# Routed experts in pairs of slots: full 128-row chunks, two 64-row remainders in two row tiles, and eight result buffers

## What is computed

```
x = x + cross_attention(layernorm(x), ctx)          # 16 heads of 16, q, k and the output normalised
h = layernorm(x)
scores = sigmoid(h @ W_gate_router)                 # 8 experts
sel = top_2(scores + expert_bias)
w = scores[sel] / sum(scores[sel])
shared = silu(h @ Wg_s) * (h @ Wu_s) @ Wd_s         # inner width 192
routed = sum over the 2 chosen e: w_e * (silu(h @ Wg[e]) * (h @ Wu[e]) @ Wd[e])   # inner width 192
x = x + shared + routed
```

## Time and profile before

| what | value |
|---|---|
| median of 3 runs | 596.49 us |
| the profiled execution | 595.83 us |
| its span, first to last instruction | 594.0 us |
| TensorE matmul busy (PE) | 502.4 us, 85% |
| VectorE busy (DVE) | 344.9 us, 58% |
| ScalarE busy (ACT) | 238.7 us, 40% |
| GpSimd busy (POOL) | 244.4 us, 41% |
| mean granted TensorE clock | 0.942 |
| L975, the `up` matmuls | 288 records, 106.1 us |
| L991, the `down` matmuls | 288 records, 74.4 us |
| L531, the scatters | 72, 111.1 us |

### The profile page before, as it was taken

One profiled execution on the slowest core, in us unless ns is written; L12 is line 12 of the kernel. 1 busy time (PEld: TensorE's weight loads), 2 busy tenths in 40 slices (PEclk: granted clock), 3 DMA queues, 4 the chain that ended last, 5 costly groups with the idle time before them and its releaser, 6 DMA issues.

```text
span 594.0 us, 10983 instructions
## 1 busy us (share of the span) xinstructions
PE 502.4 (85%) x2876; PEld 288.6 (49%) x2877; DVE 344.9 (58%) x1032; ACT 238.7 (40%) x468; POOL 244.4 (41%) x218
## 2 busy tenths in 40 slices
PE   4836989999888888856798998399999999999990
PEld 3724334444444443312454454166667666667660
DVE  5775547767888687415657933045555555555550
ACT  0255778888777777524222101022222222222210
POOL 5353411112111832361026657235565636655644
PEclk9956999999999999988799999699999999999996
DMA  8911901111111310121534652436575656664733
GB/s 284 357 44 63 290 20 37 36 38 52 37 37 36 116 66 37 55 81 46 176 100 159 216 202 77 132 49 110 75 118 93 91 99 95 98 116 75 113 52 45
DMA packets 41685, 59.78 MB, mean 101 GB/s; under 512 B 6703, under 2 KB 32047, under 8 KB 41168
## 3 DMA queue, kind: packets, MB, share of 16 engines
q0 software_dynamic: 16256, 26.49, 22.4%
q1 hardware_dynamic: 25392, 32.84, 18.3%
HBM read 31.78 MB, written 29.52 MB: 103 GB/s over the span
## 4 chain that ended last, share of the span: by engine, by line
PE 54%; DVE 16%; ACT 8%; DMA 8%; issue 6%; POOL 2%; another core or an unknown queue 2%; POOLq 1%; SPq 1%; DVEq 0%; ACTq 0%
PE bankS L975 13%; PE bankS L991 8%; PE bankV L867 5%; PE bankS L1025 5%; DMA out<-VR,attn 5%; ACT attn L623 4%; PE bankQ L742 3%; PE bankR L742 3%; PE bankV L871 2%; PE bankS L854 1%; PE bankD L964 1%; PE bankS L842 1%; PE bankQ L982 1%; POOL sorted_rows L474 1%
## 5 line engine op out<-in xcount | busy, mean ns | idle before, releaser
L531 POOL DMA_INDIRECT out<-VR,attn x72 | 111.1, 1544 | 102.5 <-DVE VR L1451 57.1
L975 PE MATMUL bankS<-experts,scores_in 128*128 x288 | 106.1, 502 | 1.8 <-issue 0.4
L474 POOL DMA_INDIRECT sorted_rows<-XR,route x64 | 63.4, 991 | 96.3 <-DVE XR L1306 46.7
L623 ACT ACTIVATE attn<-bankS,bias 128x512 f32<-128x512 f32 x128 | 81.0, 681 | 14.8 <-PE bankS L842 9.6
L991 PE MATMUL bankS<-experts,scores_in 96*128 x288 | 74.4, 380 | 0.1
L975 PEld LDWEIGHTS bankS<-experts,scores_in 128*128 128x128 f32 x288 | 52.9, 193 | 34.2 <-issue 10.1
L867 PE MATMUL bankV<-attn,VS 128*32 128x512 f32 x256 | 65.7, 637 | 4.3 <-DVE OTT L1213 2.9
L707 ACT ACTIVATE scores_in<-bankS 128x192 f32<-128x192 f32 x72 | 23.8, 330 | 112.2 <-PE bankS L975 106.6
L869 PE MATMUL bankD<-attn,ON 128*32 128x512 f32 x256 | 65.7, 637 | 0.0
L410 POOL DMA_DIRECT2D x_in<-in_xT x13 | 9.6, 736 | 114.9 <-PE bankQ L742 113.9
L1436 DVE TENSOR_TENSOR scores_in<-scores_in,bankS 128x192 f32<-128x192 f32 x72 | 25.5, 354 | 51.3 <-ACT scores_in L707 45.4
(11 more groups left out here) (254 smaller groups left out, 865.4 us busy)
## 6 DMA issues: line engine op xcount, KB each, us to landing
VS<-sorted_rows SPq DMA_DIRECT2D x72, 130.0 KB
x_cols<-X2T SPq DMA_DIRECT2D x16, 256.0 KB, 2.2
scores_in<-x_cols SPq DMA_DIRECT2D x16, 256.0 KB
out<-X POOLq DMA_DIRECT2D x8, 512.0 KB
x_in<-in_xT POOLq DMA_DIRECT2D x15, 256.0 KB, 3.6
experts<-in_wgu SPq DMA_DIRECT2D x2, 1536.0 KB, 8.8
X<-in_x SPq DMA_DIRECT2D x1, 2048.0 KB, 16.5
experts<-in_wd SPq DMA_DIRECT2D x2, 768.0 KB, 15.8
```

The source lines that it names most:

```text
L474: pool.indirect_dma_start(sorted_rows.rearrange("s p r -> (s p) r"), bass.IndirectOffsetOnAxis(ap=index, axis=0), rows, None, bounds_check ...
L531: pool.indirect_dma_start(out, bass.IndirectOffsetOnAxis(ap=dest[:, i:i + 1], axis=0), y_out[:, i % 4], None, bounds_check=B * N + SPARE - ...
L623: act.activation(Pb[:, u % 2, c, :], bankS[:, c % GH, :], ACT.Exp, bias=bias[:, b, GH * g + c:GH * g + c + 1] if c < GH else biasR[:, b, g ...
L975: last = pe.matmul(gate_bank(k)[:, 0:2 * F], x_col[:, k, c * P:(c + 1) * P], rhs, start=(c == 0), stop=(c == KC - 1))
```

## The change

Two slots are one pair h (slots 2h and 2h+1 of the quad). The inner features of a slot are cut as 128 + 64, not as 96 + 96. `h_in` of a pair is 384 columns wide: 128 of the even slot, the 64 last features of the even and of the odd slot side by side, and 128 of the odd slot. So a pair is turned by 3 transposes of 128 x 128 instead of 4 of 128 x 96. The 64 last features of the even slot come out on partitions 0 to 63, those of the odd slot on 64 to 127. `down(h)` runs one full matmul for each slot, and then the two 64-row matmuls in two row tiles, with the remainder of each expert's `Wd` copied beforehand by ScalarE (`rest_weights`) to `wd_rest`.

One VectorE copy of 128 x 384 takes the place of two of 96 x 256. `inner` of an odd slot is two instructions (64 and 128 columns). The results get eight buffers, in two turns of four, so that `result(k)` waits for the scatter of two quads back; the loop body on VectorE holds two quads (`quads_in_turn`). TensorE gets a wait for `f_h` before `up(2)` and `up(3)`.

The order on TensorE becomes up 0, up 1, up 2, turn 0, up 3, down 0, transposes, turn 1, transposes, down 1. The order on VectorE becomes inner 0, inner 1, columns 0, inner 2, inner 3, result 0, result 1, columns 1, places, result 2, result 3.

```diff
+            def rest_weights(a, k):
+                h, rows = k // 2, slice(P // 2 * (k % 2), P // 2 * (k % 2) + P // 2)
+                if not isinstance(a, int) or a >= 1:
+                    act.wait_ge(f_y["e"], 2 * a + (h - 1))
+                    aside(act)
+                e_ = act.value_load(etile[0:1, ds(4 * a + k, 1)], min_val=0, max_val=E - 1)
+                act.activation(wd_rest[rows, h], wd_sb[rows, 1, ds(e_, 1), :].rearrange("p o d -> p (o d)"), ACT.Copy).then_inc(f_wr, 1)
...
                         act.activation(act_g[:, k], gate_bank(k)[:, 0:F], ACT.Silu).then_inc(f_si[kind], 1)
+                        rest_weights(a, k)
...
-            for k in range(FC):
-                sp.dma_start(wd_sb[0:FP, k], wd[k * FP:(k + 1) * FP]).then_inc(w_in, 16)
+            sp.dma_start(wd_sb[:, 0], wd[0:P]).then_inc(w_in, 16)
+            for r in range(2):
+                sp.dma_start(wd_sb[r * P // 2:(r + 1) * P // 2, 1], wd[P:F]).then_inc(w_in, 16)
...
+                    def turn(h):
+                        bank = (bankQ, bankR)[h]
+                        pe.wait_ge(f_h[kind], 4 * a + (2 * h + 2))
+                        for t in range(2):
+                            pe.transpose(bank[:, t * P:(t + 1) * P], h_in[:, h, 2 * P * t:2 * P * t + P], id32[:, :])
+                        pe.transpose(bank[:, 2 * P:3 * P], h_in[:, h, P:2 * P], id32[:, :]).then_inc(f_ht[kind], 1)
+
+                    def down(h, e_):
+                        half = P // 2
+                        pe.wait_ge(f_hc[kind], 2 * a + (h + 1))
+                        pe.wait_ge(f_wr, 4 * a + (2 * h + 2))
+                        if h >= 1 or not isinstance(a, int) or a >= 1:
+                            pe.wait_ge(f_yd[kind], 4 * a + 2 * h)
+                        for t in range(2):
+                            rhs = wd_sb[:, 0, ds(e_[t], 1), :].rearrange("p o d -> p (o d)")
+                            pe.matmul(down_bank(t), h_col[:, h, t * P:(t + 1) * P], rhs, start=True, stop=False)
+                        for t in range(2):
+                            rows = slice(half * t, half * t + half)
+                            last = pe.matmul(down_bank(t), h_col[rows, h, 2 * P:3 * P], wd_rest[rows, h], start=False, stop=True)
+                        last.then_inc(f_y[kind], 1)
...
                     for k in range(4):
+                        if k >= 2:
+                            pe.wait_ge(f_h[kind], 4 * a + (k - 1))
                         up(k, e_[k])
                         if k < 3:
                             e_[k + 1] = expert(4 * a + (k + 1))
+                        if k == 2:
+                            turn(0)
+                    down(0, e_[0:2])
                     if more(a, tiles):
                         transposes(a + 1, 0)
+                    turn(1)
                     if more(a, tiles):
                         transposes(a + 1, 1)
+                    down(1, e_[2:4])
...
+                        if k % 2 == 0:
+                            last = dve.tensor_tensor(h_in[:, k // 2, 0:F], act_g[:, k], gate_bank(k)[:, F:2 * F], ALU.mult)
+                        else:
+                            dve.tensor_tensor(h_in[:, k // 2, F:2 * P], act_g[:, k, P:F], gate_bank(k)[:, F + P:2 * F], ALU.mult)
+                            last = dve.tensor_tensor(h_in[:, k // 2, 2 * P:2 * F], act_g[:, k, 0:P], gate_bank(k)[:, F:F + P], ALU.mult)
+                        last.then_inc(f_h[kind], 1)
+
+                    def columns(h):
+                        dve.wait_ge(f_ht[kind], 2 * a + (h + 1))
+                        aside(dve)
+                        dve.tensor_copy(h_col[:, h], (bankQ, bankR)[h][:, 0:2 * F]).then_inc(f_hc[kind], 1)
...
                     def result(k):
-                        dve.wait_ge(f_y[kind], 4 * a + (k + 1))
-                        if not isinstance(a, int) or a >= 1:
-                            dve.wait_ge(y_st[k], BASE + 16 * a)
+                        dve.wait_ge(f_y[kind], 2 * a + (k // 2 + 1))
+                        if not isinstance(a, int) or a >= 2:
+                            dve.wait_ge(y_st[k], BASE + 16 * a - 16)
...
+                    inner(3)
+                    result(0)
+                    result(1)
                     columns(1)
```

More of the change, by code:

```diff
@@ L73, in quads, with quads_in_turn @@
     body(tiles // 4 - 1)
+def quads_in_turn(eng, tiles, body):
+    body(0, 0)
+    with eng.Fori(0, (tiles // 4 - 2) // 2) as b:
+        body(2 * b + 1, 1)
+        body(2 * b + 2, 0)
+    body(tiles // 4 - 1, 1)
 def more(a, tiles):
@@ L179, in build @@
         xs_col, hs0, hs1, gs0, gs1 = views(scores_in[:, :], (2, 4, D), (2, 4, P), (2, 2, P), (4, P), (4, P))
[L180 to L183, removed]
+        x_col, act_g, h_in, h_col, wd_rest = views(scores_in[:, :], (4, D), (4, F), (2, 2 * F), (2, 2 * F), (2, D))
+        x_row, = views(VS[:, :, :, :].rearrange("p b h d -> p (b h d)"), (4, ROW))
         bankS = ps("bankS", [P, GH, 512])
@@ L284, in build @@
         e_dst = sem("e_dst")
+        f_wr = sem("f_wr")
         e_chain = sem("e_chain")
@@ L731, in _ @@
                 shared(a)
+            act.wait_ge(routed, 1)
+            act.wait_ge(w_in, 16 * (KC + 3))
             columns(0)
@@ L1430, in ffn, with four @@
             def ffn(kind, tiles):
[L1431 removed]
+                def four(a, turn):
                     def inner(k):
                         dve.wait_ge(f_si[kind], 4 * a + (k + 1))
[L1434 to L1440 removed]
+                        if not isinstance(a, int) or a >= 1:
+                            dve.wait_ge(f_ht[kind], 2 * a + (k // 2 - 1))
+                        if k % 2 == 0:
[6 more added lines that the diff above has]
+                        dve.wait_ge(f_ht[kind], 2 * a + (h + 1))
                         aside(dve)
[L1442 removed]
+                        dve.tensor_copy(h_col[:, h], (bankQ, bankR)[h][:, 0:2 * F]).then_inc(f_hc[kind], 1)
                     def result(k):
[L1445 to L1447 removed]
+                        dve.wait_ge(f_y[kind], 2 * a + (k // 2 + 1))
+                        if not isinstance(a, int) or a >= 2:
+                            dve.wait_ge(y_st[k], BASE + 16 * a - 16)
                         dve.wait_ge(e_dst, 2 * a + (k // 2 + 1))
@@ L1456, in four @@
                     inner(2)
+                    inner(3)
+                    result(0)
+                    result(1)
                     columns(1)
-                    result(0)
-                    inner(3)
-                    columns(2)
-                    result(1)
-                    columns(3)
-                    result(2)
                     if more(a, tiles):
                         places(a + 1)
+                    result(2)
                     result(3)
@@ L1515, in _ @@
             places(0)
-            quads(dve, SLOTS, ffn("e", SLOTS))
+            quads_in_turn(dve, SLOTS, ffn("e", SLOTS))
 _OUT = (B, N, D)
```

23 lines of the change are left out of this document (5 added, 18 removed).

## The result

The changed kernel takes 598.85 us, the kernel before 596.08 us (medians of 20 runs each). The ratio is 1.0042, with a 95% interval from 1.0026 to 1.0057: slower by about 2.5 us. The forecast was slower by 8.3 us. The sign was right. The size was not, and neither was most of the place: of the 2.5 us that the two traces differ by, 0.6 lie in quads 0 to 14 and 1.8 in quad 15, where the prediction expected no change.

A forecast was written before the change was run, and what follows sets the result against it. TensorE was taken to set the pace through quads 0 to 14: +0.63 us a quad, +9.5 us over 15, less 1.2 for the buffers, makes +8.3 us. Forecast 604.8 us, range 595 to 612.

The forecast's parts named there:

- the price of a quad: Routed stage: each quad changes by -0.42 + 0.93 + 0.12 = +0.63 us, +9.5 us over 15 quads.
- the wait at `down(1)`: TensorE waits for VectorE's result 0, result 1, columns 1: 2.14 us less 1.21 of cover, 0.93 us a quad.
- the 0.34 us lost at the boundary: Rest of an undisturbed quad's 10.74 us beyond 10.40 of TensorE's pieces, lost at its boundary and `turn(0)`; kept unchanged.
- the fixed end: After the results of quad 15 appear, the chain of scatter landings has a fixed length: no change.
- What bounds the kernel; 15 periods count: TensorE, busy 139.0 of 141.0 us in quads 2 to 14, sets the pace; its changes count over 15 periods.
- Transposes and down matmuls: TensorE, each quad: two transposes fewer gain 0.22 us, `down` pairs of 1.64 instead of 1.74 us gain 0.20.
- The third rival: VectorE's instructions don't overlap: the wait before the second `down` is 0.46 us longer, 611.7 us in all; chance 0.12.
- The wait before `up(2)`: TensorE waits for inner 0, then another wait and the expert's registers follow: 0.12 us new a quad.
- The weight load: Grows from 1.5 to 2 MB but is issued during attention, far ahead of first use: costs nothing.
- Buffers: Eight result buffers remove the waits for a scatter's landing in quads 9 and 10: 1.2 us gained once.
- ScalarE, turn 0: ScalarE's four `rest_weights` copies a quad fit its free time, and an up covers `turn(0)`'s longer inner 1: both nothing.
- the second: Rival: the wait before the second `down` eats the gain and no more, 595 to 597 us; chance 0.12.

The follow-up runs named there:

- e7: The changed kernel with GpSimd's two register loads for a scatter moved ahead of its waits; ratio 1.0017 to the kernel before.
- e8: The kernel before with GpSimd's register loads for a scatter moved ahead of its waits; ratio 0.9993 to the kernel before.
- e3: The changed kernel with the remainders as two matmuls over all 128 rows instead of two row tiles; ratio 1.0125 to the kernel before.
- e5: The changed kernel with columns 1 copied by ScalarE instead of VectorE; ratio 1.0014 to the kernel before.
- e6: The changed kernel with columns 1 on ScalarE and turn 1 ahead of both groups of transposes; ratio 0.9955 to the kernel before.
- e13: The kernel before with 0.5 MB more of down weights loaded, into partitions that nothing reads; ratio 1.0016 to the kernel before.
- e1: The kernel before with eight result buffers and nothing else of the change; ratio 0.9969 to the kernel before.
- e12: The changed kernel with ScalarE copying only 16 of the 256 columns of the down weights' remainders; ratio 1.0044 to the kernel before.

## Why the prediction was wrong

The step that failed is the price of a quad: +0.63 us in the sum, +0.13 in the trace, over 15 quads 7.5 us too much. Two of its terms were mis-sized: the wait at `down(1)`, 0.93 us where 0.59 was measured, and the 0.34 us lost at the boundary, which was carried over though 0.25 of it went away. A second step failed the other way: the fixed end, put at no change, grew by 1.8 us. That the sign came out right is therefore partly luck. With the quads as measured and the end as predicted, the sum would have been 15 x 0.13 - 1.2 = +0.8 us, which nobody could have told from no change.

By its steps:

- *What bounds the kernel; 15 periods count.* Right for TensorE. Wrong in "after that the chain of landings has a fixed length": it has one from scatter 60 on, but scatter 60 starts 2.1 us behind its own result. The prediction looked at scatter 63 and not at scatter 60, which starts 8.5 us into the quad, behind a result that ends at 6.3; about 1.1 of the 2.2 us between are the register loads that queue behind the wait (e7, e8). Results in pairs come 1.9 us later in a quad (7.8 instead of 5.9), so +1.8 us were missing.
- *Transposes and down matmuls.* Right: -0.22, and 1.59 and 1.69 for the pairs. An estimate by the factor of up to two in "TensorEngine Tiling (Array Packing)" of the Trainium skill, section Theoretical Speedup, is 1.39; the measured gain of the tiles over full matmuls is 0.14 of 1.73 at best (e3).
- *The wait at `down(1)`.* The mechanism was right and is shown by e5 and e6; the size was not. From TensorE's going on to the second `down` it is 1.84 us in place of 2.14. Result 0 starts 0.37 and not 0.55 us after it. The steps between VectorE's instructions (0.36 and 0.40 in quad 8, 0.36 and 0.34 in quad 9; forecast 0.34 each) and the copy (0.56, forecast 0.54) were about as forecast, TensorE's restart is 0.15 (0.17). The 0.20 for two more waits and registers on TensorE were not there. With a cover of 1.25 (transposes 0.49, turn 0.33, transposes 0.43) the wait is 0.59 us, not 0.93. The third rival did not come about: result 1 starts 0.36 us after result 0, which lasts 0.42. The section that it cites for the other outcome ("VectorE: DVE Perf Modes" of the Trainium skill, The DRAIN you can't avoid) also says that a next instruction that is not held starts earlier, which the prediction left out.
- *The wait before `up(2)`.* Three ups take 480.27 - 476.15 = 4.12, 0.25 over 3 x 1.29. Of these 0.10 were there before (two ups in 474.64 - 471.96 = 2.68), so 0.15 are new where 0.12 was forecast: right. The prediction's 474.55 for the end of up 1 is a sum of prices; the modelled end in the earlier trace rows is 474.80.
- *The 0.34 lost at the boundary.* This was carried over unchanged, and that was the second term that failed. Of the old 0.34 us, 0.25 was the pause between the last `down` and the next `up`: 482.69 - 481.57 = 1.12 for a `down` of 0.87 (kernel before, end of quad 8).

```profile
481.57 1.03 PE L991 MATMUL bankS<-experts,scores_in 96*128 x4
...
482.69 1.55 PE L975 MATMUL bankS<-experts,scores_in 128*128 x4
```

After the change the next `up` follows the 64-row matmuls of the last pair after 487.01 - 486.38 = 0.63 us, as the transposes follow those of the first (0.64), with no such pause. Some 0.1 us of the 0.34 is left. My guess is that a pair of 1.69 us, behind a wait, gives TensorE's queue the time for the loop's branch and the next register load; no run tested it.

- *The weight load.* Priced at nothing; e13 shows no cost, but leaves room for up to 0.4%.
- *Buffers.* Right: 1.2 forecast, e1 gives 1.8 (0.4 to 3.3 by its interval); its other quads are 0.05 shorter too.
- *ScalarE, turn 0.* Right, at nothing (e12).

The sum with what was measured: -0.42 + 0.63 (1.84 less the prediction's cover of 1.21) + 0.15 - 0.25 = +0.11 us a quad, where the quads show 0.13; 15 x 0.13 = 2.0; less 1.2; plus 1.8 for the late results: 2.6 us. Of the rivals, the second had the quad nearly right ("the wait eats the gain and no more") and would have been the better forecast of the quads; it too had no change at the end.

## What to carry to other kernels

When two units of work are joined so that one engine needs fewer instructions, write down what the other engines now do one behind the other between the two halves, and move one of these to an idle engine: here the joined form lost 0.4% with three VectorE steps in the gap and won 0.45% with two, once its turn also stood ahead of the transposes. Where a consumer's chain ends the kernel, ask how late in its period each unit is delivered, not only how long the period is. And try a queue's register loads ahead of its waits: in e7 this brought scatter 60 1.1 us closer to its result. But read the trace again afterwards, as work that moves can meet other work: in e8 the same edit gained nothing that could be measured.

## What the hardware showed that was not expected

The two-column copy that VectorE makes at the boundary of quads takes 0.17 us, but 0.50 when it starts at a certain moment of a GpSimd scatter. In e8, where the scatters moved, GpSimd's ran from 450.23 to 451.77 and the copy starts 0.51 us behind its start:

```profile
450.23 1.54 POOL L531 DMA_INDIRECT out<-VR,attn  x1 [0.65 <-issue]
...
450.74 0.50 DVE L1421 CAST attn<-VS 128x2 f32 x1
...
450.87 0.38 DVE L1422 TENSOR_TENSOR attn<-VS,attn 128x2 f32<-128x2 f32 x1
```

In the kernel before, the same copy starts 0.47 us behind the start of the scatter, also within its time, and is not longer:

```profile
450.34 1.54 POOL L531 DMA_INDIRECT out<-VR,attn  x1 [0.62 <-DVE VR L1451]
...
450.81 0.17 DVE L1421 CAST attn<-VS 128x2 f32 x1
```

So it is not enough that the two overlap. Ten such copies of e8 start 0.51 to 0.52 us behind a scatter's start and take 0.50 each, so they end 1.02 us behind it. An eleventh, in quad 0, starts as late and takes 0.16, so the moment is not all. In the kernel before, copies that start up to 0.49 us behind a scatter's start take 0.17. The ten quads of e8 that follow such a copy are the ones that are 0.2 us longer (10.91 to 10.96 us, and 10.68 for quad 16, which takes 10.48 before). In e1 a copy of 0.50 us in quad 1 was followed by a quad of the usual length. The way is in the trace: around the start of quad 5, with the copy at 0.50, result 3 and the next inner 0 start 0.21 us later than around quad 4, where it takes 0.17. Over a whole kernel that copy's durations are

```profile
L1421 DVE CAST attn<-VS x36: 158/169/501, 380.3 to 570.1; 128x2 f32 x32, 128x2 int32<-128x2 f32 x4
```

(least, median, most, in ns) before, and 157/169/277 after. Ten quads at 0.2 us are 2 us, so this accounts for most of the gain that e8 missed. Why the two collide was not tested.
